# Query splitting spread over two engines, and loads and last products put elsewhere, in a two-layer gated cross-attention kernel

## The chip, the cores and the metric

The kernel runs on one core of one Trainium2 chip. The metric is the device time of one execution in microseconds (us). The engines are called PE (TensorE, with its weight loads listed as PEld), DVE (VectorE), ACT (ScalarE), POOL (GpSimd) and SP (SyncE, which here only issues DMAs). "ACTq" and "SPq" in the profile's rows are the DMA-issuing instructions of ACT and SP.

## The reference

Sixteen samples of 56 queries (width 128) attend to 1500 context rows each, through two layers. Each layer is a gated cross-attention with 16 heads of width 8, followed by a gated mixture of 8 experts:

```
q, k, v = x @ Wq + bq, ctx @ Wk + bk, ctx @ Wv + bv        # split into 16 heads of 8
w   = softmax(q k / sqrt(8))          # layer 1: scores where mask == 0 are -1e9
x   = x + tanh(g_xattn[l]) * (concat(w v) @ Wo + bo)
xf  = layernorm(x)                    # also ahead of q
gate = top-2 of 8, scores softmax (layer 0) or sigmoid (layer 1), normed to sum 1
x   = x + tanh(g_ffn[l]) * sum_e gate[e] * (gelu(xf @ W1[e] + b1[e]) @ W2[e] + b2[e])
```

Layer 0's experts have 512 hidden columns, layer 1's have 64 and there is a shared expert beside them.

## The kernel before

The work is one long pipeline over `NB = 32` batches (16 samples in each of 2 layers), written out as steps `s = -1 .. 35`. A step has 12 places `kt = 0 .. 11`, and every engine's program is an order written by hand over `s` and `kt`; engines meet only through semaphores. In step `s` PE finds the row maxima of batch `s` (24 products into `pMX`, three banks, read by DVE at L1112), computes the scores of batch `s-1` (from kt 3, `pST`, exponentials by ACT at L817), multiplies them with the values (`pO`, L1251), and projects keys of batch `s+1` and values of batch `s` (`pKV`). Everything else of PE goes through one PSUM bank, `pF`, in the order that `f_uses(s)` lists: each use waits until DVE has read the use before it (semaphore `f_free`). The uses that matter here are

- `qT` and `q` (odd steps up to 29, for the next two batches: `has_q`): PE transposes the normalised queries `xnq` and a row `keep` (ones in layer 0, in layer 1 whether a sample has any valid key), and DVE copies both (L1009, L1010). PE then multiplies with Wq and adds the bias through `keepT` (L1393, L1394). DVE makes from the result, for each of the two heads of a pair, the f16 high part (`qhi`, L1020, twice) and the f16 rest (`qlo`, L1022, twice), masked by `head_of`.
- `y` (odd steps, kt 7): the attention's output product (L1335), after `q`. DVE then adds the residual, takes the layer norm's statistics (L1043 to L1049), POOL makes `xnf` (L719 to L724), and PE transposes it at kt 9 (`xT`, L1339) for the experts (`h0` and on, L1404 or L1408).
- `ct` (kt 1): the row maxima of batch `s-1` as f16 rows. SP copies them into `qexp` (L554), and PE's first score tile of that batch, at kt 3, waits for it (`shift_in`).
- `y0` to `y3`, `yb`: the experts' second products and their biases; `gT` the transposed gates. In the last steps (33 = `sums_last`, 34, and 35 = `ends`) these run with nothing beside them.

The f16 parts of the keys are POOL's (`low_part`, three chunks a step, L650 and L652), and so are the parts of the context (L758, L760). In steps 2 and 3 it also makes the low parts of layer 0's first expert weights.

SP issues all loads and copies of the steady state, in program order: in a step first `ct`'s two copies, then key chunk 2, then expert weights (`expert_weights`), the context load (750 KB), key chunk 0, the queries (`queries`, into `qmax`), key chunk 1, and last `late_loads`. In step -1 key chunk 0 stands before the context load, and ACT issues the first queries at kt 5.

## Time and profile before

| | |
|---|---|
| median of 3 runs | 983.31 us (979.77 to 984.18) |
| profiled execution | 990.22 us, of which 988.1 us are the span of the trace |
| mean granted clock of PE in it | 0.954 of full speed |
| busy share of the span | PE 89%, PEld 64%, DVE 72%, ACT 60%, POOL 53% |
| busy us | PE 875.2, DVE 709.9, ACT 591.9, POOL 524.0 |
| DMA queue of SP (q1) | 102.07 MB, 44.2% of 16 engines |

Times within the trace count from the start of the span. The profiled execution is one run and about 7 us longer than the median of the timed ones, so a sum of its durations is compared with its own time, and the difference is carried over to the median.

### The profile page before, as it was taken

To read this page: it belongs to the slowest core of one execution; us is meant where nothing else is said; L and a number is where in the kernel's file an instruction comes from. 1 tells how busy PE (TensorE), PEld (TensorE's weight loads), DVE (VectorE), ACT (ScalarE), POOL (GpSimd) and SP (SyncE) were. 2 spreads that over 40 slices of the span, in tenths; PEclk is the share of its full clock that TensorE was granted. 3 is DMA by queue.
4 is the path that set the end of the run, shared out by engine and by line. 5 is a ranking of instruction groups with operands and counts; after the bars stand their busy time and mean duration, and the time that the engine had idled before them with its cause. 6 is when DMAs were issued, how large, how long until landed. Compare 5 with 4: busy or idle time off the path is not lost.

```text
span 988.1 us, 33064 instructions
## 1 busy us (share of the span) xinstructions
PE 875.2 (89%) x13280; PEld 630.3 (64%) x13280; DVE 709.9 (72%) x1600; ACT 591.9 (60%) x1085; POOL 524.0 (53%) x701
## 2 busy tenths in 40 slices
PE   3888899889898988899999999999999999999975
PEld 1355667667676766667667676666666666666653
DVE  5764885777868586786867858687787878787713
ACT  2254666575665757557575575757666666766560
POOL 5545754536535454463655556677566666662202
PEclk9885998999999999999999999999999999999985
DMA  6243442122222122222666646676786767666200
GB/s 161 84 140 116 136 129 76 53 85 82 77 84 76 47 72 74 84 86 70 122 120 136 147 85 152 135 160 141 147 154 130 161 115 151 134 128 114 44 2 19
DMA packets 103556, 104.49 MB, mean 106 GB/s; under 512 B 28442, under 2 KB 97388, under 8 KB 103404
## 3 DMA queue, kind: packets, MB, share of 16 engines
q1 hardware_dynamic: 101986, 102.07, 44.2%
q8 instruction: 105, 1.72, 0.9%
q10 hardware_dynamic: 1418, 0.32, 0.2%
q14 instruction: 47, 0.39, 0.2%
HBM read 35.89 MB, written 0.46 MB: 37 GB/s over the span
## 4 chain that ended last, share of the span: by engine, by line
PE 56%; DVE 23%; ACT 11%; issue 7%; POOL 2%; DMA 1%; ACTq 0%; SPq 0%; POOLq 0%; DVEq 0%
PE pO L1251 12%; DVE mx L1112 11%; PE pST L1230 10%; PE pMX L1272 9%; PE pKV L1308 5%; PE pKV L1317 5%; ACT P L817 3%; PE pF L1370 3%; PE pF L1404 3%; ACT HR L826 2%; ACT L817 2%; PE pF L1374 2%; DVE HR L994 1%; DVE rden L1038 1%; ACT V L849 1%
## 5 line engine op out<-in xcount | busy, mean ns | idle before, releaser
L1112 DVE TENSOR_REDUCE mx<-pMX 112x1 f32<-112x500 f32 x768 | 489.4, 667 | 110.2 <-PE pMX L1272 106.9
L817 ACT ACTIVATE P<-pST 125x448 f32<-125x448 f32 x768 | 389.5, 542 | 242.8 <-PE pST L1230 239.0
L1230 PE MATMUL pST<-qexp,kop 50*128 50x112 f16 (+2 forms) x3072 | 271.0, 217 | 24.3 <-ACT P L817 15.8
L1272 PE MATMUL pMX<-kop,qmax 48*112 48x500 f16 (+1 forms) x768 | 279.7, 409 | 9.8 <-DMA qmax<-qlo 6.5
L1230 PEld LDWEIGHTS pST<-qexp,kop 50*128 50x128 f16 (+2 forms) x3072 | 185.3, 102 | 104.0 <-ACT P L817 43.1
L1251 PE MATMUL pO<-P,V 125*18 125x112 f32 x6144 | 192.6, 268 | 4.9 <-issue 4.8
L1251 PEld LDWEIGHTS pO<-P,V 125*18 125x18 f32 x6144 | 141.4, 100 | 40.1 <-issue 22.7
L650 POOL CAST khi<-kfull 128x500 f16<-128x500 f32 x96 | 57.7, 601 | 162.3 <-ACT kfull L844 162.1
L1272 PEld LDWEIGHTS pMX<-kop,qmax 48*112 48x112 f16 (+1 forms) x768 | 99.0, 132 | 54.8 <-DVE mx L1112 17.1
L652 POOL TENSOR_TENSOR klo<-kfull,khi 128x500 f16<-128x500 f32 x96 | 109.0, 1135 | 7.8
L760 POOL TENSOR_TENSOR Clo<-C,Chi 128x500 f16<-128x500 f32 x93 | 105.7, 1136 | 7.5
L849 ACT ACTIVATE V<-pKV 125x512 f32<-125x512 f32 x96 | 57.7, 601 | 43.4 <-PE pKV L1317 40.4
L844 ACT ACTIVATE kfull<-pKV,bkp 128x500 f32<-128x500 f32 x48 | 32.5, 677 | 68.0 <-PE pKV L1308 64.4
L1317 PE MATMUL pKV<-Whi,Chi 128*128 128x128 f16 (+1 forms) x384 | 72.0, 225 | 1.3 <-ACT V L849 1.1
L1370 PE MATMUL pF<-w2a,HR 128*112 128x128 f32 x512 | 62.9, 280 | 10.2 <-ACT HR L826 7.9
L1317 PE MATMUL pKV<-Whi,Clo 128*128 128x128 f16 (+1 forms) x384 | 71.4, 223 | 0.0
L1317 PE MATMUL pKV<-Wlo,Chi 128*128 128x128 f16 (+1 forms) x384 | 71.4, 223 | 0.0
L1076 DVE TENSOR_TENSOR ysc<-pF,gate 112x512 f32<-112x512 f32 x32 | 22.1, 692 | 67.8 <-PE pF L1370 49.3
L1370 PEld LDWEIGHTS pF<-w2a,HR 128*112 128x112 f32 x512 | 59.3, 181 | 15.0 <-issue 10.0
L758 POOL CAST Chi<-C 128x500 f16<-128x500 f32 x93 | 55.8, 600 | 12.8 <-PE pKV L1317 10.7
L708 POOL TENSOR_TENSOR OM<-OM,rden 128x112 f32<-128x112 f32 x32 | 13.5, 422 | 86.0 <-DVE rden L1038 86.0
L994 DVE TENSOR_TENSOR HR<-pF,W 128x448 f32<-128x448 f32 x64 | 39.8, 622 | 22.9 <-PE pF L1404 22.2
(161 smaller groups left out, 1199.3 us busy)
## 6 DMA issues: line engine op xcount, KB each, us to landing
C<-in_ctxT SPq DMA_DIRECT2D x31, 750.0 KB, 6.4
kop<-maskop SPq DMA_DIRECT2D x48, 437.5 KB
kop<-khi SPq DMA_DIRECT2D x192, 62.5 KB
kop<-khi SPq DMA_DIRECT2D x96, 125.0 KB
kop<-klo SPq DMA_DIRECT2D x96, 62.5 KB
kop<-klo SPq DMA_DIRECT2D x48, 125.0 KB
maskin<-in_mask SPq DMA_DIRECT2D x8, 656.2 KB, 5.3
qexp<-qmax SPq DMA_DIRECT2D x16, 182.0 KB
```

Of the source, the lines that this page charges most:

```text
L650: nc.gpsimd.tensor_copy(khi[:, cols], kfull[:, c, :]).then_inc(khi_done, 1)
L652: nc.gpsimd.tensor_tensor(klo[:, cols], kfull[:, c, :], khi[:, cols], ALU.subtract).then_inc(klo_done, 1)
L758: nc.gpsimd.tensor_copy(Chi[:, s % 2, cols], C[:, cols]).then_inc(chi_done, 1)
L760: nc.gpsimd.tensor_tensor(Clo[:, s % 2, cols], C[:, cols], Chi[:, s % 2, cols], ALU.subtract).then_inc(ctx_split, 1)
L817: nc.scalar.activation(P[0:KP, slot, h * 4 * T:(h + 1) * 4 * T], pST[0:KP, h, 0:4 * T], ACT.Exp, scale=EXP_SCALE).then_inc(exp_done, 1)
L849: nc.scalar.activation(V[0:KP, s % 2, 4 * c:4 * c + 4, :, 0:PR].rearrange("k t p i -> k (t p) i"), pKV[0:KP, :].rearrange("k (m i) -> k m ...
L1112: nc.vector.tensor_reduce(mx[:, s % 2, c, p:p + 1], pMX[0:T, m % 3, 0:CW], AX.X, ALU.max).then_inc(max_done, 1)
L1230: mm = nc.tensor.matmul(pST[0:keys.stop - keys.start, h, i * T:(i + 1) * T], kop[rows, b, slot, keys], qexp[rows, b, slot, :, :].rearrange ...
L1251: mm = nc.tensor.matmul(pO[32 * g:32 * g + VW, r * T:(r + 1) * T], V[0:KP, b, tile, p, :], P[0:KP, tile % RING, p * T:(p + 1) * T], start= ...
L1272: nc.tensor.matmul(pMX[0:T, m % 3, 0:CW], qmax[rows, b, slot, :, :].rearrange("r j q -> r (j q)"), kop[rows, b, slot, c * CW:(c + 1) * CW] ...
L1317: mm = nc.tensor.matmul(pKV[0:rows, i * D:(i + 1) * D], x_[:, s % 2, cols], m[:, l, 1, :], start=(k == 0), stop=(k == 2))
L1370: mm = nc.tensor.matmul(o, HR[:, F0C * e + c, :], w2a[:, e, c, :], start=(c == 0), stop=(c == F0C - 1))
```

## The change

For the queries, DVE masks both heads in one operation into a new f32 tile `qfull` and frees `pF` with it. POOL makes `qhi` (a cast) and `qlo` (a subtraction) from `qfull`, between its key chunks 1 and 2, and what issues the queries' copies waits for POOL (`q_split`). The row `keep` is transposed and copied in step -1 and for layer 1 alone. Loads: the small ones (`b2x`, `ws2b`, `bs1b`) go from SP's step 1 to ACT's step 0, kt 8; the first mask (656 KB) from SP's step 1 to its step 3; in step -1 the context load stands before key chunk 0. In steps 33 to 35 the experts' second products go into the three banks of `pMX`, under semaphores of their own, in another order; `XF` gets two buffers.

```diff
+def masks_queries(s):
+    return s == -1 or s + 1 >= B
...
     if has_q(s):
-        uses += [(2, "qT", 2), (3, "q", 2)] if s < 0 else [(4, "qT", 2), (6, "q", 2)]
+        uses += [(2 if s < 0 else 4, "qT", 1 + masks_queries(s)), (3 if s < 0 else 6, "q", 1)]
     if has_end(s) and not sums_last(s):
-        uses += [(1, "y2", 0), (2, "y3", 1), (3, "yb", 1)]
+        uses += [(1, "y2", 0), (2, "y3", 1), (3, "yb", 1)] * (not ends(s))
...
-    if sums_last(s):
-        uses += [(5, "y0", 0), (5, "y1", 1), (6, "yb", 1)]
     if has_a(s):
-        uses += [(7, "y", 1)] + [(7, "y2", 0), (7, "y3", 1)] * sums_last(s)
-        uses += [(9, "xT", 1), (10, "h0", 1), (10, "lg", 1), (11, "h1", 1)]
+        uses += [(6 if sums_last(s) else 7, "y", 1), (9, "xT", 1)]
+        uses += [(10, "lg", 1), (10, "h0", 1)] if sums_last(s) else [(10, "h0", 1), (10, "lg", 1)]
+        uses += [(11, "h1", 1)]
...
+def last_uses(s):
+    if sums_last(s):
+        return [(5, "y0", 0), (5, "y1", 1), (7, "y2", 0), (7, "y3", 1), (7, "yb", 1)]
+    if s == NB + 2:
+        return [(10, "y0", 0), (10, "y1", 1)]
+    if ends(s):
+        return [(1, "yb", 1), (2, "y2", 0), (2, "y3", 1)]
+    return []
...
 # SP
             def late_loads(s):
-                if s == 1:
-                    sp.wait_ge(init_w, 4)
-                    sp.dma_start(b2x[0:NE, 0, :], b2_0).then_inc(f_in, 16)
-                    sp.dma_start(b2x[:, 1, :], b2_1).then_inc(f_in, 16)
-                    sp.dma_start(ws2b[:, :], ws2).then_inc(f_in, 16)
-                    sp.dma_start(bs1b[:, :], bs1).then_inc(f_in, 16)
+                if s == 3:
                     sp.dma_start(maskin[:, :], mask[0]).then_inc(mask_in, 16)
...
                 expert_weights(s)
-                if s == -1:
-                    key_chunk(st, 1, 0)
...
                 if has_k(s):
-                    if s >= 0:
-                        key_chunk(st, 1, 0)
+                    key_chunk(st, 1, 0)
                     if has_q(s) and s >= 0:
-                        sp.wait_ge(f_free, st.at(lambda s: upto(f_uses, s, "q", True)))
+                        sp.wait_ge(q_split, 2 * q_count(s) + 2)
...
 # POOL, after low_part(st, 1), the OM and ON products and mask_part(st, 2)
+                if has_q(s):
+                    pool.wait_ge(f_free, upto(f_uses, s, "q", True))
+                    apart(pool)
+                    if s > 0:
+                        pool.wait_ge(qmax_in, q_total(s))
+                        apart(pool)
+                    nc.gpsimd.tensor_copy(qhi[:, :, :, :], qfull[:, :, :, :]).then_inc(q_split, 1)
+                    pool.wait_ge(q_split, 2 * q_count(s) + 1)
+                    nc.gpsimd.tensor_tensor(qlo[:, :, :, :], qfull[:, :, :, :], qhi[:, :, :, :], ALU.subtract
+                                            ).then_inc(q_split, 1)
                 low_part(st, 2)
...
 # ACT
                 if s == -1 and kt == 5:
-                    act.wait_ge(f_free, upto(f_uses, s, "q", True))
+                    act.wait_ge(q_split, 2)
                     queries(act, 0)
...
+                if s == 0 and kt == 8:
+                    act.dma_start(b2x[0:NE, 0, :], b2_0).then_inc(f_in, 16)
+                    act.dma_start(b2x[:, 1, :], b2_1).then_inc(f_in, 16)
+                    act.dma_start(ws2b[:, :], ws2).then_inc(f_in, 16)
+                    act.dma_start(bs1b[:, :], bs1).then_inc(f_in, 16)
...
 # DVE
-                        q = pF[:, 0:T].rearrange("p (b q) -> p b q", b=2)
-                        own = head_of[:, layer_of(s + 1), :]
-                        for j in range(2):
-                            link(nc.vector.tensor_scalar(qhi[:, :, j, :], q, own[:, j:j + 1], None, ALU.mult))
-                        for j in range(2):
-                            nc.vector.scalar_tensor_tensor(out=qlo[:, :, j, :], in0=q, scalar=own[:, j:j + 1],
-                                                           in1=qhi[:, :, j, :], op0=ALU.mult, op1=ALU.subtract
-                                                           ).then_inc(f_free, 1)
+                        q = pF[:, 0:T].rearrange("p (b q) -> p b q", b=2).unsqueeze(2).broadcast_to([128, 2, 2, S])
+                        own = head_of[:, layer_of(s + 1), :].unsqueeze(1).unsqueeze(3).broadcast_to([128, 2, 2, S])
+                        nc.vector.tensor_tensor(qfull[:, :, :, :], q, own, ALU.mult).then_inc(f_free, 1)
...
 # PE, small(use): the last products go to pMX
+                    if is_last(s, use):
+                        into, signal = pMX[:, 2 if use == "yb" else int(use[1]) // 2, :], last_ready
+                        if sums_last(s) and use == "y0":
+                            pe.wait_ge(max_done, NMAX * NB)
+                        if s == NB + 2 and use == "y0":
+                            pe.wait_ge(last_free, before(last_uses, s, True))
```

## Rows read from the trace of the kernel before

**Rows 1.** The page's chain that ended last: shares of the span by engine.
```profile
PE 56%; DVE 23%; ACT 11%; issue 7%; POOL 2%; DMA 1%; ACTq 0%; SPq 0%; POOLq 0%; DVEq 0%
```
**Rows 2.** Instructions grouped by line, shapes apart: total busy us, mean ns | idle before.
```profile
L652 POOL TENSOR_TENSOR klo<-kfull,khi 128x500 f16<-128x500 f32 x96 | 109.0, 1135 | 7.8
...
L650 POOL CAST khi<-kfull 128x500 f16<-128x500 f32 x96 | 57.7, 601 | 162.3 <-ACT kfull L844 162.1
...
L994 DVE TENSOR_TENSOR HR<-pF,W 128x448 f32<-128x448 f32 x64 | 39.8, 622 | 22.9 <-PE pF L1404 22.2
...
L1010 DVE COPY keepT<-pF 1x112 f32<-1x112 f32 x16 | 4.0, 252 | 0.0
...
L1054 DVE TENSOR_TENSOR xflo<-pF,xfhi 128x112 f16<-128x112 f32 x8 | 2.2, 274 | 0.3
```
**Rows 3.** Waits: who waited for whom, us in total, times, longest.
```profile
PE pF L1335 <- DVE qlo L1022: 9.5, 14, 0.9
```
**Rows 4.** Chain in order of time, step 23: start us, us, what.
```profile
707.24 0.41 PE pF L1394 x2
...
709.04 0.69 PE pF L1335 x4
```
**Rows 5.** Timeline of POOL, step 11: start us, us, instruction [idle before <-releaser].
```profile
352.47 1.13 POOL L652 TENSOR_TENSOR klo<-kfull,khi 128x500 f16<-128x500 f32 x1
355.38 0.23 POOL L719 TENSOR_SCALAR vef<-mvf 112x1 f32<-112x1 f32 x1 [1.78 <-DVE mvf L1049]
```
**Rows 6.** Timeline of SP, end of step 1 and start of step 2.
```profile
69.09 0.49 SPq L490 DMA_DIRECT2D b2x<-in_b  x1
...
71.19 0.59 SPq L494 DMA_DIRECT2D maskin<-in_mask  x1
71.89 1.47 SPq L554 DMA_DIRECT2D qexp<-ct  x2
```
**Rows 7.** Timeline of PE, step 2, kt 3.
```profile
77.61 0.61 PE L1230 MATMUL pST<-qexp,kop 50*128 50x112 f16 x8 [5.79 <-issue]
```
**Rows 8.** Windows: us, busy us of each engine (instructions), PE's clock, DMA share, GB/s.
```profile
57.00:71.80 14.80, 13.41 (x251) 9.47 (x250) 12.01 (x26) 10.15 (x21) 6.88 (x8) 1.00 0.39 112
...
77.60:94.50 16.90, 16.75 (x181) 10.87 (x182) 8.21 (x14) 8.79 (x18) 7.67 (x10) 0.50 0.40 130
```
**Rows 9.** Timeline of SP at the end of step 3 and of step 4's `ct`.
```profile
124.66 2.40 SPq L529 DMA_DIRECT2D kop<-khi  x2
128.72 1.36 SPq L554 DMA_DIRECT2D qexp<-ct  x2
```
**Rows 10.** Timeline of PE, step 4, kt 3.
```profile
132.17 0.41 PE L1272 MATMUL pMX<-kop,qmax 48*112 48x500 f16 x1
```
**Rows 11.** Timeline of all engines, step -1 and start of step 0.
```profile
12.50 2.86 ACTq L467 DMA_DIRECT2D qmax<-qhi  x4
...
14.10 1.13 POOL L652 TENSOR_TENSOR klo<-kfull,khi 128x500 f16<-128x500 f32 x1
...
15.15 0.51 SPq L581 DMA_DIRECT2D C<-in_ctxT  x1
...
21.20 1.05 PE L1272 MATMUL pMX<-kop,qmax 48*112 48x500 f16 x3 [6.54 <-DMA qmax<-qlo]
```
**Rows 12.** DMA issues by line: KB each, median us from issue to landing.
```profile
out<-X SPq DMA_DIRECT2D x1, 56.0 KB, 1.6
```
**Rows 13.** Chain in order of time, steps 33 to 35: start us, us, what.
```profile
957.12 0.46 PE pF L1330 x2
...
962.63 0.71 PE pF L1354 x2
...
963.76 1.21 PE pF L1335 x4
...
968.76 0.46 PE pF L1339
...
979.63 0.70 DVE ysc L1076
```

85 lines of the change are left out of this document (59 added, 26 removed).

## The prediction

> **What bounds the kernel now.** I read the page's chain of the work that ended last first: PE 56%, DVE 23%, ACT 11% [rows 1]. So there is no single bound, and an edit is worth what it takes off that chain where it stands. Next I asked for the waits of PE. One recurs: the output product `y` waits for DVE's `qlo`, 14 times, once in each odd step from 3 to 29, for 9.5 us, 0.68 us each [rows 3]. The chain in order of time shows the place: in step 23 PE ends the query product at 707.65, the next piece of PE is `y` at 709.04, and the 1.39 us between are DVE's four query operations [rows 4]. In layer 0 the chain goes on through DVE and POOL to the experts, and POOL starts `vef` when DVE's statistics are ready, 1.78 us after it had nothing to do [rows 5].
>
> Then I looked for single long holes. The longest in the steady state is 5.79 us of idle PE in step 2, at kt 3, before the first score tile of batch 1 [rows 7]. "Issue" says that the profile names no releaser. That tile needs the copies of `ct`. SP was free for them at 69.09, but first issued five late loads, the 656 KB mask last at 71.19, and only at 71.89 the copies [rows 6], which then follow the mask in the same queue. The windows show what came behind: PE at its 2.4 GHz level before the hole (granted 1.00), at its 1.2 GHz level for 16.9 us behind it (granted 0.50), busy 16.75 of them [rows 8]. The start waits for the last `qmax<-qlo` copy until 21.20 [rows 11], and the end is one serial chain through `pF` [rows 13].
>
> **The change part by part.** Every term is in us on the profiled execution (990.22); minus is a gain.
>
> *Query operations, steps 5 to 29.* One operation of 224 columns takes the place of four. A `tensor_tensor` from PSUM takes 0.274 for 112 columns and 0.622 for 448 [rows 2], by a line between them 0.39 for 224; ends 0.27 and 0.62. With the hand-overs some 0.45 stand where 1.39 stood, so `pF` is free 0.9 earlier. PE, however, idles only 0.68 of this time; the rest is its own work, so `y` comes 0.68 earlier. POOL takes over a cast and a subtraction of 224 columns. For 500 columns it needs 0.60 and 1.135 [rows 2]. In proportion that is 0.27 + 0.51 = 0.78, at the full price 1.74. Fixed costs weigh more in short operations: I take 0.95, and 0.05 for hand-over. They stand ahead of key chunk 2, so this moves: in step 11 `klo` ended at 353.60 and `vef` started at 355.38 [rows 5]. With the pair from 351.95 (DVE's result at 351.86) to 352.95 and chunk 2's 1.8 behind it, POOL is free at about 354.8, and starts `vef` there, 0.55 earlier instead of 0.9. So layer 0's five steps (5 to 13) give 0.55 each, -2.8. In layer 1 the chain behind `y` is PE itself [rows 4], and the eight steps 15 to 29 give 0.68 each, -5.4. The pair's results are needed by the next step's first product, five places later; SP's issue waits about 0.1 longer than before, which nothing on the chain sees.
>
> *Step 1* has no `y`; behind the query operations stand the row maxima, -0.7. *Step 3* goes the other way: POOL has four expert parts there and is itself on the chain, so its pair comes on top, +1.0 (0.8 to 1.7).
>
> *Row of ones.* Six odd steps of layer 0 behind step 1 and step 1 itself lose a copy of 0.25 [rows 2] and a transposition. The copy stands between the transposition and PE's `sum`; I count 6 times 0.25, -1.5 (0 to -2.2).
>
> *Small loads to ACT.* Four issues of about 0.5 [rows 6]. ACT has nothing to do at that place of step 0 until the values' products are ready: 0. Uncovered they would cost 2.
>
> *The mask away from step 1.* With all five issues gone, `ct`'s copies are issued at about 69.2 and take 1.47. A small copy with a free queue lands 1.6 after its issue [rows 12]; the second is issued at 70.0, so both are there by 71.8, when PE asks: -5.8 for the hole. What is late next is nothing but PE's own pace. The time at half clock: 251 matmuls took 14.8 at full clock [rows 8], so the 181 of the 16.9 us would take 10.7, which is 6.2 less. As ACT and DVE don't get faster with PE, I take -5.5 (0, if the clock falls anyway, to -6.2).
>
> *The mask in step 3.* SP now issues it at 127.1, behind key chunk 1, and `ct`'s copies of step 4 at 128.72 [rows 9] queue behind it. In step 2 PE went on 6.42 after the mask's issue [rows 6, 7]. The same gives 133.5, and PE is at this tile at about 132.2 [rows 10], since four expert products fill the places before: +1.3 (0 to 4).
>
> The Trainium skill ("DMA: Bandwidth & Descriptors", "Issuing engines are not separate DMA queues") says that transfers share the same 16 DMA engines whoever issues them, so a load given to ACT saves only the issuing time. By that rule the gain is the mask's move in time and not the change of queue, and it would be as large with the small loads left on SP but for their 2 us of issue.
>
> *Start.* POOL makes the first query parts only behind key chunk 1, which it ends at 15.23, so at about 16.3; ACT's six issues, from 12.50 at 0.72 each [rows 11], start 3.8 later and end at 20.6, and behind them key chunk 2 is late too, which has slack until kt 8. But the last copy lay behind the context load issued at 15.15 [rows 11], which now is gone by then. With a landing of 1.6 after the last issue [rows 12] it is there at 21.5 to 22.3, against 20.96: +1.0 (0 to 3.8, if something else holds it).
>
> *End.* PE no longer waits for `rden`, the read of `ysc` and the bias ahead of `y`: `sum` ends at 957.58, two groups of four products of 1.2 [rows 13] follow, and `y` starts at about 960.5, not 963.76. But `y2`, `y3` and `yb` (2.5 + 1.5, the bias products being two pairs of 0.7) now stand ahead of `xT`, which so comes at 965.8, not 968.76 [rows 13]: -3.0. Behind it, dropping one read of `ysc` (0.70) and of `gateT` pays for the bias products that were moved forward. Together -3.0 (-2 to -4).
>
> Sum: -2.8 - 5.4 - 0.7 + 1.0 - 1.5 - 5.8 - 5.5 + 1.3 + 1.0 - 3.0 = -21.4, from 990.22 to 968.8. The profiled execution is 6.9 above the median of the three runs. Carried over, 983.3 - 21.4 = 962.
>
> **The rivals.** *The hole moves, or the clock stays.* The mask holds `ct` in step 4 as it did in step 2 and PE falls to half clock there, or it does so in step 2 for another reason. For it: a lull of PE was followed by the low level once [rows 7, 8]. Against it: PE gets to step 4's tile late. The 5.5 are lost: 968.
>
> *POOL becomes the bound of the odd steps.* If the pair costs 1.74, `vef` in layer 0 comes 0.2 later than before instead of 0.55 earlier, and in layer 1 PE waits for `xT` likewise. Fourteen steps lose about 1.0 of the forecast each: 976. Against it: the idle 1.78 before `vef` [rows 5].
>
> *The mask was not the cause.* The copies are late because of something the rows don't name. Then 11.3 stay: 973. Against it is only the order in the queue.
>
> *Slower.* POOL's pair alone decides it, where it is on the chain in all 14 odd steps. To lose the 21.4 and 5 more, each step must lose 1.9 more than forecast, so the pair must take some 2.9 and not 1.0: 989. Nothing in the rows is that slow at this size; the full price of 500 columns is 1.74.
> The Trainium skill ("GPSIMD Engine Reference", "4.1 Engine selection") speaks against this part: elementwise work on two inputs belongs on VectorE, being about twice as slow on GpSimd. By that rule the subtraction costs more in total busy time than it saves; whether it costs time is a question of which engine waits.
>
> *No effect.* DVE's time comes back in another wait of the same step, and the hole's in the next step: within 5 of 983.
>
> **How the numbers follow.** A measurement of this kernel tells about 0.5% (4.9) from no change. Chances: the sum as it stands 0.52 (955 to 968), clock or second hole 0.20 (968), POOL 0.14 (976), mask innocent 0.07 (973), no effect 0.04, slower 0.03. The likeliest gives 962. Upward the range takes the bounds of the clock (5.5), the start (2.8) and half of POOL's case, to 975; downward the bounds at the start, in step 4 and at the row of ones (3), `y`'s full 0.9 (3), and 3 from run to run, to 953. Faster 0.93, same 0.04, slower 0.03.
>
> **What would show it.** Right: no wait of PE for DVE before `y`; one DVE line of about 0.4 for the queries and two POOL lines summing to 0.95; no idle PE at step 2's kt 3 and a granted clock of 1.00 there; a hole of 1 to 2 at step 4's kt 3; the first row-maximum product at about 22; the last stretch from `sum` to the end shorter by 3. Wrong: POOL's `vef` released by POOL's own queue later than before; half clock in steps 2 to 4; step lengths from one step's maxima to the next's in layer 1 that stay as they are.

## The result and the profile after

The kernel after takes 967.19 us (median of 4 runs, 965.04 to 972.72); the kernel before took 983.74 on the same chip (979.77 to 985.60). The ratio is 0.985, with a 95% interval of 0.980 to 0.990: faster by 16.5 us. The predicted 962 is 5 us too low, and 967 lies in the range. The profiled execution of the kernel after took 965.04, with a span of 963.2; that of before took 990.22, with a span of 988.1. The two profiled spans lie 24.9 apart, because the one of before lies 6.5 above the median of its kernel and that of after 2 below. So I compare steps and not totals.

A step is measured from the DVE reduction `m` of one step's row maxima to that of the next. Where nothing disturbs them, equal steps agree to 0.04 us, also between kernels. Each length is from one profiled execution. The start and steps 1 to 3 scatter more: the four traces of kernels that make their first queries as the kernel after does have a start of 42.17 to 42.75. The lengths, in us:

| | before | after | difference | forecast |
|---|---|---|---|---|
| start, to the first `m` | 41.87 | 42.17 | +0.30 | +1.0 |
| step 1 | 24.87 | 24.20 | -0.67 | -0.7 |
| step 2 | 32.97 | 22.42 | -10.55 | -11.3 |
| step 3 | 25.22 | 29.03 | +3.81 | +0.75 |
| step 4 | 30.16 | 30.00 | -0.16 | +1.3 |
| steps 5 to 31 | 779.55 | 766.68 | -12.87 | -9.45 |
| of these, an odd step of layer 0 | 28.34 | 27.83 | -0.51 | -0.80 |
| an odd step of layer 1 | 28.19 | 27.71 | -0.48 | -0.68 |
| last `m` to the end | 53.42 | 48.72 | -4.70 | -3.0 |

(The forecast has the row of ones in it, -0.25 in each odd step from 3 to 13.) In steps 5 to 31 the thirteen odd steps give 5 x 0.51 + 8 x 0.48 = 6.4. The other 6.5 goes, but for 0.3 in step 31, with TensorE's clock: the trace of before shows seven stretches there at the 1.2 GHz level, one of 6.8 us and six of 3.4, and that of after four of 3.4. A step with one of 3.4 is 1.2 to 1.6 us longer than its equals, the one with 6.8 is 2.7 longer. The stretches sit elsewhere, or are absent, in kernels whose steps there are the same. Without them the differences of the table add up to 18.4, near the 16.5 of the medians.

The waits of PE and POOL after; columns: who waited for whom, us in total, times, longest.

```profile
PE pF L1391 <- POOL xnf L749: 6.3, 8, 2.6
POOL qhi L734 <- DVE qfull L1059: 15.6, 15, 4.5
POOL vef L744 <- DVE mvf L1090: 6.2, 2, 3.4
```

The wait of `y` for DVE [rows 3] is no longer among them: it was 9.5 us in 14 waits. A smaller one stands in its place. `xT` waits for POOL's `xnf` for 6.3 us in 8 waits. `vef`, for which DVE's statistics came last in step after step of before [rows 5], waits for them in two steps only. POOL in step 11, timeline:

```profile
339.00 0.37 POOL L734 CAST qhi<-qfull 128x224 f16<-128x224 f32 x1 [1.21 <-DVE qfull L1059]
339.44 0.61 POOL L736 TENSOR_TENSOR qlo<-qfull,qhi 128x224 f16<-128x224 f32 x1
340.00 0.60 POOL L665 CAST khi<-kfull 128x500 f16<-128x500 f32 x1
340.68 1.14 POOL L667 TENSOR_TENSOR klo<-kfull,khi 128x500 f16<-128x500 f32 x1
341.78 0.24 POOL L744 TENSOR_SCALAR vef<-mvf 112x1 f32<-112x1 f32 x1
```

The idle 1.78 us ahead of `vef` [rows 5] is used up; the five stand back to back. The new operations by themselves, grouped by line (total busy us, mean ns):

```profile
L1059 DVE TENSOR_TENSOR qfull<-pF,head_of 128x224 f32<-128x224 f32 x16 | 6.3, 392 | 10.3 <-PE pF L1451 10.3
...
L736 POOL TENSOR_TENSOR qlo<-qfull,qhi 128x224 f16<-128x224 f32 x16 | 9.7, 609 | 1.3
...
L734 POOL CAST qhi<-qfull 128x224 f16<-128x224 f32 x16 | 5.9, 372 | 15.6 <-DVE qfull L1059 15.6
```

The pair costs 0.98 us (0.95 estimated), the operation on DVE 0.39 (0.39).

SP at the turn from step 1 to step 2, timeline; the answer to [rows 6]:

```profile
69.75 1.37 SPq L572 DMA_DIRECT2D qexp<-ct  x2
```

The last copy of `ct` landed at 72.14, 1.7 us after the issue of the second (70.48), and PE idles 0.21 us there. In the kernel before it had landed at 77.52, 4.9 us after its issue (72.67), and PE went on at 77.61 [rows 7]. The windows of step 2, of step 3 to its stretch at half clock, and of that stretch (us, busy us and instructions of PE, PEld, DVE, ACT and POOL, then PE's clock, DMA share, GB/s):

```profile
66.40:88.80 22.40, 18.88 (x354) 12.77 (x352) 17.53 (x32) 16.59 (x34) 13.86 (x17) 1.00 0.42 125
88.80:112.00 23.20, 18.55 (x321) 12.95 (x322) 18.74 (x39) 15.09 (x30) 18.00 (x25) 1.00 0.51 147
112.00:115.40 3.40, 3.40 (x51) 2.54 (x49) 1.32 (x3) 0.55 (x1) 2.87 (x4) 0.51 0.18 50
```

PE is at its 2.4 GHz level through step 2, where the kernel before had 16.9 us at a granted 0.50 [rows 8]. Step 3, however, has 3.4 us at the 1.2 GHz level, from 111.95, which is 1.7 us behind the end of PE's longest idle time there. That idle time and its cause are in POOL's timeline of step 3 and PE's row behind it:

```profile
103.29 0.37 POOL L734 CAST qhi<-qfull 128x224 f16<-128x224 f32 x1 [0.20 <-DVE qfull L1059]
103.73 0.61 POOL L736 TENSOR_TENSOR qlo<-qfull,qhi 128x224 f16<-128x224 f32 x1
...
106.07 2.26 POOL L675 TENSOR_TENSOR w1lo<-HR,w1hi 128x512 f16<-128x512 f32 x2
108.31 0.23 POOL L744 TENSOR_SCALAR vef<-mvf 112x1 f32<-112x1 f32 x1
```
```profile
110.25 0.29 PE L1391 MATMUL pF<-ident,xnf 112*128 112x112 f32 x1 [2.60 <-POOL xnf L749]
```

PE's second longest idle time of step 3 is at its first product, which needs the query rows. SP's row of their last copies, and PE's:

```profile
86.36 1.24 SPq L490 DMA_DIRECT2D qmax<-qlo  x2
```
```profile
89.06 0.39 PE L1316 MATMUL pMX<-kop,qmax 48*112 48x500 f16 x1 [1.48 <-DVE mx L1153]
```

The row names DVE, but the last of these copies landed at 88.86, 0.20 us ahead of the product, and in the twelve kernels in which this product waits, those below included, it starts 0.20 us or 0.21 behind that landing. So I take the copy as the releaser. In the kernel before the rows landed at 95.78 and the product started at 98.35, without a wait.

The chain of the end, in order of time (start us, us, what):

```profile
937.83 1.05 PE pMX L1429 x4
938.93 1.19 PE pMX L1429 x4
940.12 1.14 PE pF L1387 x4
...
943.92 0.83 POOL xnf L749
944.75 0.14 issue
944.88 0.43 PE pF L1391
```

From the last `m` to `xT` it was 34.1 us and is 30.4.

### The profile page after: what moved, and what is told of

Its sections match the earlier page's. It is cut to its first block, busy times and chain, and to the rows that moved or that the text cites. A ratio compares the mean times of both kernels' runs of the same rounds, so it can differ in the third digit from the quotient of the medians.

```text
span 963.2 us, 33056 instructions
## 1 busy us (share of the span) xinstructions
PE 861.1 (89%) x13273; PEld 620.4 (64%) x13273; DVE 697.7 (72%) x1545; ACT 591.7 (61%) x1085; POOL 538.8 (56%) x733
## 4 chain that ended last, share of the span: by engine, by line
PE 56%; DVE 20%; ACT 11%; issue 6%; POOL 3%; ACTq 1%; DMA 1%; SPq 0%; POOLq 0%; DVEq 0%
PE pO L1295 12%; PE pST L1274 11%; DVE mx L1153 10%; PE pMX L1316 9%; PE pKV L1361 5%; PE pKV L1352 5%; ACT P L856 3%; PE pF L1425 3%; PE pF L1461 3%; ACT HR L865 2%; ACT L856 2%; DVE HR L1033 1%; ACT V L888 1%; DVE rden L1078 1%; ACT L865 1%
## 5 line engine op out<-in xcount | busy, mean ns | idle before, releaser
L1274 PE MATMUL pST<-qexp,kop 50*128 50x112 f16 (+2 forms) x3072 | 268.2, 215 | 19.8 <-ACT P L856 16.6
L1274 PEld LDWEIGHTS pST<-qexp,kop 50*128 50x128 f16 (+2 forms) x3072 | 182.8, 100 | 99.1 <-ACT P L856 42.6
L1295 PE MATMUL pO<-P,V 125*18 125x112 f32 x6144 | 189.4, 265 | 4.5 <-issue 4.4
L1295 PEld LDWEIGHTS pO<-P,V 125*18 125x18 f32 x6144 | 139.2, 99 | 39.1 <-issue 19.8
L1425 PE MATMUL pF<-w2a,HR 128*112 128x128 f32 x512 | 61.2, 275 | 10.6 <-ACT HR L865 8.0
L1117 DVE TENSOR_TENSOR ysc<-pF,gate 112x512 f32<-112x512 f32 x28 | 19.4, 692 | 58.0 <-PE pF L1425 49.2
```

Source lines behind the costliest of these rows:

```text
L1274: mm = nc.tensor.matmul(pST[0:keys.stop - keys.start, h, i * T:(i + 1) * T], kop[rows, b, slot, keys], qexp[rows, b, slot, :, :].rearrange ...
L1295: mm = nc.tensor.matmul(pO[32 * g:32 * g + VW, r * T:(r + 1) * T], V[0:KP, b, tile, p, :], P[0:KP, tile % RING, p * T:(p + 1) * T], start= ...
L1425: mm = nc.tensor.matmul(o, HR[:, F0C * e + c, :], w2a[:, e, c, :], start=(c == 0), stop=(c == F0C - 1))
```

## The experiments

Twelve kernels ran. Their step lengths stand together, since most verdicts are read from them (us; "odd 0" and "odd 1" are an undisturbed odd step of either layer; the total is the median, with the number of runs). "wait 3" is PE's wait at the first product of step 3, "low 3" the time at the 1.2 GHz level in step 3. e1 to e4, e5 to e8 and e9 to e12 ran on three chips, each with the kernel before beside them (medians 983.3, 982.5 and 981.7), so ratios compare better than totals:

| | start | 1 | 2 | 3 | wait 3 | low 3 | 4 | odd 0 | odd 1 | end | total |
|---|---|---|---|---|---|---|---|---|---|---|---|
| before | 41.87 | 24.87 | 32.97 | 25.22 | 0 | 0 | 30.16 | 28.34 | 28.19 | 53.42 | 983.7 (4) |
| after | 42.17 | 24.20 | 22.42 | 29.03 | 1.48 | 3.4 | 30.00 | 27.83 | 27.71 | 48.72 | 967.2 (4) |
| e1_mask_only | 42.59 | 26.88 | 22.16 | 31.17 | 3.60 | 10.2 | 30.00 | 28.35 | 28.19 | 52.41 | 981.9 (10) |
| e2_small_only | 43.06 | 26.96 | 21.83 | 30.40 | 2.77 | 10.2 | 30.00 | 28.34 | 28.19 | 53.14 | 980.3 (10) |
| e3_q_only | 45.03 | 26.64 | 28.85 | 29.54 | 0 | 6.8 | 30.00 | 27.86 | 27.72 | 52.91 | 983.1 (10) |
| e4_dve_splits_two | 39.14 | 23.87 | 21.87 | 30.25 | 2.29 | 10.2 | 30.00 | 27.83 | 27.71 | 48.54 | 963.4 (4) |
| e5_w1lo_behind | 42.60 | 26.69 | 21.60 | 28.46 | 2.84 | 3.4 | 31.75 | 27.82 | 27.71 | 48.23 | 971.0 (1) |
| e6_weights_late | 39.93 | 23.67 | 22.79 | 28.47 | 0.17 | 3.4 | 30.00 | 27.83 | 27.71 | 48.62 | 968.1 (1) |
| e7_dve_splits_all | 40.56 | 26.89 | 21.59 | 28.40 | 2.61 | 3.4 | 30.00 | 30.11 | 28.83 | 47.72 | 996.1 (4) |
| e8_pair_behind | 40.26 | 23.60 | 23.54 | 32.36 | 2.05 | 13.7 | 30.00 | 27.54 | 27.48 | 48.75 | 989.5 (10) |
| e9_mask_back | 42.75 | 26.60 | 22.98 | 29.70 | 2.11 | 6.8 | 30.00 | 27.83 | 27.71 | 48.23 | 964.3 (1) |
| e10_small_back | 42.42 | 23.60 | 26.47 | 30.83 | 0.37 | 10.2 | 29.99 | 27.82 | 27.71 | 48.48 | 970.4 (1) |
| e11_three_in_two | 40.24 | 23.54 | 21.81 | 29.23 | 0.72 | 3.4 | 30.00 | 27.82 | 27.71 | 47.74 | 964.1 (6) |
| e12_three_on_dve | 39.64 | 24.44 | 21.99 | 26.08 | 1.53 | 0 | 31.68 | 27.99 | 27.88 | 48.49 | 962.5 (4) |

Step 1 comes in two lengths, 23.5 to 24.9 and 26.6 to 27.0. They go with TensorE's clock: the stretch at 1.2 GHz that begins at the end of the start is over by 57.3 us or earlier in before, after, e4, e6, e8 and e12 (13.7 long), and at 65 to 67 in e1, e3 and e9 (20.5 long). Kernels with the same step 1 stand on both sides (after and e5), so I don't put it down to an edit. It matters all the same, because the longer step 1 brings PE later to step 2's first tile of batch 1, where the hole of the kernel before is.

The length of step 3 follows "low 3" closely: 25.2 and 26.1 with none, 28.4 to 29.2 with 3.4 us, 29.5 and 29.7 with 6.8, 30.3 to 31.2 with 10.2, 32.4 with 13.7. Waits and the low clock go together here, and this order alone doesn't say which brings which. In e5 and e12 a stretch of 3.4 us falls in step 4, which is 1.7 longer, so steps 3 and 4 have to be read together.

**e1_mask_only and e2_small_only** put one half each of the moved loads into the kernel before.

```
 e1:            if s == 1: ... four small loads
-                   sp.dma_start(maskin[:, :], mask[0])
+               if s == 3:
+                   sp.dma_start(maskin[:, :], mask[0])
 e2:            if s == 1:
-                   ... four small loads
                    sp.dma_start(maskin[:, :], mask[0])
+ ACT, step 0, kt 8:  the four small loads
```

> The kernel before with only the first mask load moved from SP's step 1 to its step 3; the four small loads stay ahead of ct's copies. Theory (the mask ahead of ct's copies in SP's queue made the hole of step 2): the copies are issued 0.7 us earlier, at about 71.2, with a free queue, and PE goes on at about 73.7, so the hole shrinks from 5.8 to about 2 us; if PE keeps its high clock behind it, step 2 is 8 to 9 us shorter than before (32.97 us in the trace before), otherwise 4. Time 973 to 976 (980 if the clock falls). Rival (the hole has another cause, or SP's issue time of all five loads is what counts): the hole stays at 5 us or more and the time within 1 us of before. Step 4 should be no longer than before, or up to 1.3 us if the mask now delays ct there.

> The kernel before with only the four small loads moved to ACT's step 0; the mask stays at SP's step 1, ahead of ct's copies. Theory (mask in the queue): the mask is issued at about 69.1 and PE goes on some 6.4 us later, at 75.5; the hole is 3.7 us instead of 5.8 and PE still falls to its low clock, so step 2 is 2 us shorter and the time 981 to 982. Rival (SP's issue time is what counts): the hole nearly vanishes, step 2 is 8 to 10 us shorter and the time 974.

In both traces the hole is nearly gone (0.53 and 0.20 us), and step 2 is 22.16 and 21.83 for 32.97. Part of this is when PE arrives: step 1 has its longer length here, and PE reaches the tile at 74.55 and 75.10, for 71.82 in before. e10 and e9 below have the same loads ahead of `ct` as e1 and e2, with holes of 2.50 and 1.35. So these two traces don't show that either half alone cures a PE that comes at 71.8. And though step 2 gained more than was expected of either, the totals gained little: e1's 981.9 is 2 over the most that its theory allowed, and e2's 980.3 is near its theory's, with a step 2 like its rival's. e1 stands at a ratio of 0.9996 to before (0.9965 to 1.0028), e2 at 0.9966 (0.9930 to 1.0001). Of e1's 10.8 us in step 2, 6.0 come back in step 3 and 2.0 in step 1; e2 loses 5.2 in step 3, 2.1 in step 1 and 1.2 at the start (the part in step 1 goes with the clock there and is not put down to the edit). The waits of PE in step 3 of e1 show what took the place of the hole, a wait for the query rows at the step's first product:

```profile
PE pMX L1273 <- DMA qmax<-qlo: 3.6, 1, 3.6
```

In e1 SP's queue issues with no gap over 0.2 us from 70.02 until these rows are out at 92.1; in the kernel before it stood still from 80.8 to 86.1. The stall was cover for SP's queue. The second thing lost is clock: e1 has 10.2 us at 1.2 GHz from 92.2, e2 from 92.8.

**e3_q_only** put the query operations alone into the kernel before (DVE's one operation, POOL's pair and their waits; not the context load, the small loads, the mask, the row of ones or the end).

> The kernel before with only the query split changed (one masking operation on DVE, cast and subtraction on POOL). Theory (POOL's pair of 1.05 us now ends last in every odd step): the start of vef is 0.48 us earlier relative to the query operation's start in each odd step from 5 to 29, whatever the layer, and each of these steps 0.48 us shorter, -6.2 together; step 3 longer by 1.2 us or more; the first row maximum product 1 to 4 us later, as the context load still stands in the way of the last query copy. Time 979 to 982. Rival (PE's wait for pF was the whole effect, as forecast): 0.68 us in the steps of layer 1, -8.2 and 977.

The odd steps shorten by 0.48 in layer 0 and 0.47 in layer 1, the same in both layers. What else moved gives it back: the start is 3.2 us longer (2.4 against e1, whose start is that of before), step 1 is 1.8 longer, and step 3 is 4.3 longer while step 2 is 4.1 shorter. Step 2 is shorter with all five loads in place because PE, after the longer step 1, reaches the tile at 76.75 and waits 3.56 us, not 5.79. Step 3 is the other thing to note: there is no wait for the query rows, and POOL's pair alone brings PE's wait for `xnf` from 0.5 to 2.6 us, with 6.8 us at 1.2 GHz behind it. The ratio is 0.9987 (0.9954 to 1.0021). The pair's cost at the start is 2.4 to 3.2 us when the context load is where it was. The kernel after, with the loads reordered, has +0.3. Against the odd steps of the kernel after (27.83 and 27.71) those of e3 are 0.03 and 0.01 longer. In layer 1 the row is copied in both, so what the row of ones gives in layer 0 is 0.03 at most.

**e4_dve_splits_two** is the kernel after, with DVE making the parts itself in steps -1 and 3, from `qfull`.

```
-                if has_q(s):                                   # POOL
+                if has_q(s) and s not in (-1, 3):
 ...
                 nc.vector.tensor_tensor(qfull, q, own, ALU.mult)
+                if s in (-1, 3):
+                    nc.vector.tensor_copy(qhi, qfull)
+                    nc.vector.tensor_tensor(qlo, qfull, qhi, ALU.subtract)
```

> The changed kernel, where in steps -1 and 3 DVE makes the f16 parts itself, from qfull (a cast and a subtraction behind the masking), and POOL does in all other odd steps. Theory (in step 3 POOL's pair is on the chain, 1.2 us, and the gap of PE behind it drops the clock): step 3, 29.03 us in the trace after, falls to 25.5 to 27.5; in step -1 the query copies are issued 3 us earlier, and the first row maximum product starts 2 to 3 us earlier unless key chunk 0, which lands behind the context load, ends last. Time 2 to 5 us under the changed kernel, 962 to 965. Rival (step 3 is long for the C load, the expert loads or DVE): step 3 stays at 29 and the time at that of the changed kernel.

The total is 963.4, a ratio of 0.9791 (0.9730 to 0.9852), within the 962 to 965 expected, but of the two reasons given only one came true. The start is 3.0 shorter. Step 3 is not: 30.25. Taking POOL's pair out of step 3 was not enough, because a wait of 2.3 us for the query rows, one of 1.5 for DVE's maximum and 10.2 us at half clock stand there:

```profile
PE pMX L1328 <- DMA qmax<-qlo: 2.3, 1, 2.3
PE pMX L1328 <- DVE mx L1165: 1.5, 1, 1.5
```

**e5_w1lo_behind** takes, in the kernel after, the two `w1lo` operations of step 3 from ahead of `vef` to behind `xnf`.

```
                 low_part(st, 2)
-                expert_low(st, 2); expert_low(st, 3)
+                if s != 3: expert_low(st, 2); expert_low(st, 3)
                 ... vef, rsf, xnf
+                if s == 3: expert_low(st, 2); expert_low(st, 3)
```

> The kernel after, with one thing moved: in step 3 GpSimd makes the low parts of experts 6 and 7 (w1lo, 1.15 us each) behind vef, rsf and xnf and not ahead of them. In the kernel after, step 3 is 29.03 us long where it was 25.22 before, TensorE stands 2.6 us ahead of xT behind GpSimd's xnf, and vef starts 2.2 us after the last DVE operation it needs (mvf ends at 105.70, vef starts at 108.31). Theory, GpSimd bounds step 3: xT comes 2.1 to 2.3 us earlier against the step's start and step 3 falls to about 26.8 (25.9 to 27.2). Rival, the length of step 3 is set at its entry, by query rows and clock: TensorE's wait ahead of xT goes but the step stays at 28.5 to 29.5 because another wait behind it takes its place. Steps 5 to 29 stay at 27.8 and 30.1 in layer 0.

It gave 0.57 instead of 2.2, and step 4 is 1.75 longer, with a stretch at 1.2 GHz in it. The idle time ahead of `xT` did go, from 2.60 to 0.4. The expert products wait for the very `w1lo` that was moved. The wait for the query rows at the step's first product is not new, but it is 2.84 for 1.48, though up to there the two programs are the same: the rows landed 2.7 us after their last issue, not 1.9.

```profile
PE pMX L1320 <- DMA qmax<-qlo: 2.8, 1, 2.8
...
PE pF L1465 <- POOL w1lo L675: 1.6, 1, 1.6
```

So moving POOL's work inside the step did not help here: the rival was nearer the truth. It is one trace, and what differs in it without an edit behind it (the landing, the clock) is as large as the effect that was looked for.

**e6_weights_late** issues, in e4, the three expert weight loads of step 2 behind the query rows.

```
-                expert_weights(s)
+                if s != 2: expert_weights(s)
                 ... context load, key chunk 0, query rows
+                if s == 2: expert_weights(s)
```

> The version in which VectorE makes the parts of steps -1 and 3 (e4), with one thing moved: in step 2 SyncE issues the three loads of expert weights (1.5 us of issuing, 768 KB) behind the key chunk and the query rows and not ahead of them. In e4 the queue of SyncE issues without a gap from 66.6 to 84.5, and the first pMX product of step 3 waits 2.3 us for the query rows; in the run with the mask alone moved it waits 3.6 us. Theory, the stall of step 2 was cover for SyncE's queue, and without it the query rows of step 3 are late by what is issued ahead of them: they leave 1.5 us earlier and land 1.5 to 2.5 us earlier, the wait at the entry of step 3 falls from 2.3 to under 1 us, and step 3 falls from 30.25 to 28 to 29. Rival, the landing is what is slow, by the bytes of the context load and the weights, or the wait is replaced by one for VectorE's maximum: the wait stays over 1.5 us or step 3 stays over 29.5.

Step 3 falls from 30.25 to 28.47, as expected, and the wait at its first product from 2.29 to 0.17. e11, which has the weights late too, has 0.72. In the nine kernels with a hole of 1.35 us or less and the weights in their old place it is 1.5 to 3.6, in e10, with a hole of 2.5, 0.37, and in before and e3, with holes of 5.8 and 3.6, nothing. So SP's queue is what makes this wait, and the stall was what covered it. PE's waits for DVE are now the longest of step 3 (2.6 us in five waits).

**e7_dve_splits_all** is e4 with the parts made by DVE in every step, again from `qfull`.

> The kernel after, but VectorE makes the two f16 parts in every step, from the masked queries, with one cast and one subtraction over all 224 columns; GpSimd makes none. Theory, the pair on GpSimd bounds vef of each odd step (0.98 us ahead of klo, vef right behind klo), and the pair is no gain over three wide operations on VectorE: vef comes at +3.3 to +3.7 us from the start of the masking operation (after: +3.44), the steps 5 to 29 keep their length within 0.3, the start is 3 us shorter (39.1 for 42.2), and the total is 962 to 965, 2 to 5 us under the kernel after. Rival, VectorE bounds: its queue carries 0.6 to 0.9 us more in each odd step, as it did before the change, vef comes at +3.9 as before, the odd steps go back to 28.3 in layer 0, 28.2 in layer 1 (+0.5 x 13), and the total is 967 to 970.

996.1 us, a ratio of 1.0146 (1.0076 to 1.0217): 29 over the kernel after, far worse than the theory's 962 to 965 and the rival's 967 to 970. The odd steps are 30.11 and 28.83 where nothing else disturbs them. The timelines of DVE and of POOL in step 11 show why.

```profile
356.88 0.39 DVE L1063 TENSOR_TENSOR qfull<-pF,head_of 128x224 f32<-128x224 f32 x1 [0.59 <-PE pF L1463]
357.31 0.64 DVE L1068 CAST qhi<-qfull 128x224 f16<-128x224 f32 x1
357.98 1.29 DVE L1070 TENSOR_TENSOR qlo<-qfull,qhi 128x224 f16<-128x224 f32 x1
```
```profile
357.21 0.60 POOL L669 CAST khi<-kfull 128x500 f16<-128x500 f32 x1 [0.89 <-ACT kfull L887]
357.89 1.13 POOL L671 TENSOR_TENSOR klo<-kfull,khi 128x500 f16<-128x500 f32 x1
```

DVE's cast ends 0.14 us behind POOL's `khi`, its subtraction 0.25 behind POOL's `klo`: each is stretched until POOL's operation is over. Step -1 has the same subtraction with POOL idle:

```profile
12.02 0.39 DVE L1070 TENSOR_TENSOR qlo<-qfull,qhi 128x224 f16<-128x224 f32 x1
```

In the fifteen others, all beside `klo`, it takes 1.21 to 1.30 us. The Trainium skill ("SBUF — State Buffer", "SBUF: two separate sides") says that a DVE operation in a two-port mode, or one with two SBUF inputs beside a GpSimd operation that reads SBUF, contends with GpSimd for one pair of ports, an exclusive lock: whichever starts first has it for its whole length, and the other waits. The trace agrees, with 1.29 us beside POOL for 0.39 alone.

**e8_pair_behind** puts POOL's pair, in e4, behind `xnf` (except in steps -1 and 3, where DVE makes it).

> The version in which VectorE makes the parts of steps -1 and 3 (e4), with one thing moved: in the other odd steps GpSimd makes the pair behind vef, rsf and xnf and not ahead of the last key chunk's parts. Theory, the pair is on the path of GpSimd ahead of vef: with it gone vef waits for VectorE's mvf (+3.06 us from the masking operation) and starts at about +3.1, not +3.44, xT comes 0.3 to 0.4 us earlier and each of the 12 odd steps gets 0.3 to 0.4 shorter, 27.5 for 27.8, total 4 us under e4 (958 to 961). Rival, the query rows leave 2.5 to 3 us later, SyncE's queue and the first pMX products of the next step wait for them: the even steps get longer by 1 to 3 us each, total 975 or more.

Both halves of the expectation happened. The odd steps are shorter by 0.29 and 0.23, as POOL's bound before `vef` says. The even steps are longer, 31.1 for 30.25 in layer 0, 39.85 for 33.98 in step 16 and 26.5 to 27.7 for 25.58 in layer 1, and the total is 989.5, a ratio of 1.0054 (1.0016 to 1.0093). The query rows now leave late, and what stands behind them in SP's queue too. In step 11 SP issues them from 348.33; m of that step is at 353.22. In the kernel after the same issue starts at 340.43 and `m` is at 349.86, so the margin shrank from 9.4 to 4.9 us. Behind them key chunk 1 and `ct` shift likewise. Between 607 and 690 us (steps 20 to 22) PE waits 4.2 us, in two waits, for scores whose copies are late: both products start 0.09 us behind the landing of `ct`'s last copy.

```profile
PE pST L1286 <- issue: 4.2, 2, 2.1
```

**e9_mask_back and e10_small_back** take the kernel after and put back one half each of the loads in step 1, ahead of `ct`'s copies.

```
 e9:   late_loads:
-                if s == 3:
+                if s == 1:
                    sp.dma_start(maskin[:, :], mask[0])
 e10:  late_loads:
+                if s == 1:
+                    ... four small loads      (gone from ACT)
                 if s == 3:
                    sp.dma_start(maskin[:, :], mask[0])
```

> The kernel after, with the mask load back in step 1, ahead of the copies of ct in SyncE's queue; the four small loads stay on ScalarE in step 0. In the kernel before, the last copy of ct landed at 77.52, 4.9 us after its issue began (72.67), and TensorE stood until 77.61; in the kernel after it landed at 72.14, 1.7 us after its issue (70.48), and TensorE never waited. With the mask as the only late load in the queue (the run with the small loads alone moved) it landed 1.9 us after its issue. Theory of the prediction, the mask's packets are served ahead of the copies of ct: the last copy lands 4 us or more after its issue, TensorE stands 2 to 4 us at key tile 3 of step 2, and step 2 is 24.5 to 27 us (22.42). Rival, it takes the mask and the small loads together, by issue time and landing: the copies land in 1.7 to 2.2 us and step 2 stays within 0.7 us of 22.4.

> The kernel after, with the four small loads back in step 1 in SyncE's queue, ahead of the copies of ct; the mask stays in step 3. Theory of the prediction, their 2.4 us of issuing matter little beside the mask: the copies of ct are issued 1 to 2 us later than in the kernel after (69.75), land in under 2.2 us, and step 2 is 22.4 to 23.4. Rival, the small loads fill the queue: step 2 is over 24.5 us. In step 3 the query rows land about as much later as the queue is behind, up to 2.4 us, so its length may grow by 0 to 2.4.

SP's timeline of e9, then PE at the place of the hole:

```profile
69.91 1.31 SPq L512 DMA_DIRECT2D maskin<-in_mask  x1
71.91 1.37 SPq L572 DMA_DIRECT2D qexp<-ct  x2
```
```profile
75.78 0.37 PE L1274 MATMUL pST<-qexp,kop 50*128 50x112 f16 x7 [1.35 <-issue]
```

The same of e10, and its windows around the wait:

```profile
70.81 0.60 SPq L516 DMA_DIRECT2D bs1b<-in_bs  x1
71.53 1.45 SPq L578 DMA_DIRECT2D qexp<-ct  x2
```
```profile
74.08 0.61 PE L1275 MATMUL pST<-qexp,kop 50*128 50x112 f16 x8 [2.50 <-issue]
```
```profile
66.00:73.30 7.30, 5.10 (x99) 3.17 (x96) 5.58 (x11) 4.13 (x8) 2.13 (x3) 1.00 0.20 59
73.30:80.10 6.80, 5.88 (x65) 3.74 (x65) 2.73 (x6) 3.19 (x7) 1.84 (x2) 0.50 0.23 72
```

With the mask alone ahead of them the copies landed 3.0 us after their issue (75.69 for 72.64), 0.24 behind the mask itself (75.45), and PE waited 1.35; step 2 is 0.56 longer. (In before the mask landed at 76.89 and the copies at 77.52.) Neither expectation of e9 is met: the landing lies between the two. For e10 the rival's is, a step 2 over 24.5. With the small loads alone they landed 1.7 after their issue (74.00 for 72.30), but were issued 1.8 later than in the kernel after, PE waited 2.50, fell to 1.2 GHz for 6.8 us, and step 2 is 4.05 longer. One difference between the two has to be kept in mind: step 2 began at 66.0 in e10 and at 69.4 in e9, so PE reached the tile earlier in e10 (71.59) than in e9 (74.44). So the hole of the kernel before has two causes, late issue by the small loads and late landing by the mask, and the first was not in the prediction as a cause of its own. PE came at 71.82 in before, nearly as in e10, so an estimate from e10's 2.50 leaves some 3.3 of the 5.8 us to the mask; no trace shows that share by itself. Step 3 is longer than in the kernel after as well, by 0.67 and 1.80.

**e11_three_in_two and e12_three_on_dve** let DVE make the parts straight from PSUM, so that no operand pair comes from SBUF: one operation for `qhi` with the mask broadcast, two for `qlo`. e11 does so in steps -1 and 3 (and has the late weights of e6), e12 in every step, with no pair on POOL at all.

```
 e12:  link(nc.vector.tensor_tensor(qhi, q, own, ALU.mult))          # q: PSUM, broadcast
       for j in range(2):
           nc.vector.scalar_tensor_tensor(out=qlo[:, :, j, :], in0=q1, scalar=own1[:, j:j + 1],
                                          in1=qhi[:, :, j, :], op0=ALU.mult, op1=ALU.subtract)
```

> The kernel after, with two changes meant to take back what step 3 and the start lost: in steps -1 and 3 VectorE makes the parts itself, straight from PSUM, in three operations (qhi with the broadcast mask, then qlo for each head group), and in step 2 SyncE issues the expert weights behind the query rows. Elsewhere GpSimd's pair stays. Theory, parts made from PSUM don't suffer where parts made from SBUF did (qhi 0.72 and qlo 1.30 us in step 3 of the run with the late weights): the three take 1.0 to 1.1 us, the start is 39.0 to 40.0 (42.17 after), step 3 is 27 to 28 (29.03 after), steps 5 to 29 as in the kernel after but for changes of clock, total 959 to 963. Rival, step 3's length is set at its entry and by the clock, and what is saved there is given back: step 3 stays over 28.4 and the total is within 2 us of the version of e4 (963.4).

> The kernel after, but GpSimd makes no parts at all: in every query step VectorE makes them from PSUM in three operations (one broadcast for qhi, two for qlo), where the kernel before used four. The run in which VectorE made both parts from SBUF had odd steps of 30.1 in layer 0 and 28.8 in layer 1, with a subtraction of 1.29 us that ended 0.2 us after GpSimd's klo. Theory, it was reading both operands from SBUF while GpSimd ran that cost, and not VectorE's load: here the three take 1.0 to 1.1 us, vef starts at +3.6 to +3.7 from the first of them (after +3.44, before +3.93), the odd steps are 28.0 to 28.2 in layer 0 and 27.9 to 28.1 in layer 1, 0.2 to 0.3 over the kernel after, the start is 39 to 40, and the total is 965 to 970. Rival, VectorE's queue bounds as soon as it makes the parts: odd steps of 28.8 or more and a total of 975 or more.

e12 takes 962.5 us, a ratio of 0.9806 to before (0.9757 to 0.9855), 2.5 under the least that was expected; e11 964.1, a ratio of 0.9808 (0.9768 to 0.9848). The two intervals overlap with that of the kernel after (0.980 to 0.990), so it is the steps that set e12 apart. Its three operations take 1.00 us from first to last, in DVE's timeline of step 3:

```profile
99.67 0.39 DVE L1049 TENSOR_TENSOR qhi<-pF,head_of 128x224 f16<-128x224 f32 x1 [0.67 <-PE pF L1445]
100.09 0.58 DVE L1051 SCALAR_TENSOR_TENSOR qlo<-pF,head_of,qhi 128x112 f16<-128x112 f32 x2
```

Its odd steps are 27.99 and 27.88, at the low edge of what was expected and only 0.16 longer than with GpSimd's pair, and its start is 2.5 shorter. Its step 3 is 2.95 shorter, but its step 4 is 1.68 longer, since the stretch of 3.4 us at 1.2 GHz falls there (from 116.19): steps 3 and 4 together are 1.27 shorter. In e11 step 3 did not come down: 29.23, with one wait of 1.8 us ahead of a score product at 93.00 and 3.4 us at half clock from 94.9. Its theory failed for step 3; the start is 40.24, 0.2 over what it said. That is the rival of e11, as is the total within 2 us of e4's. What set that wait was not tried.

## Why the prediction was right, point by point

**Right in direction and size.** The hole of step 2 and its clock gave 10.6 of the forecast 11.3, and the pair on POOL and the operation on DVE cost what was estimated (POOL's subtraction takes 609 ns, where DVE took 0.39 us for it in e7 with POOL idle). Step 1 gave 0.67 of 0.7, but among the seven traces of after and of its variants with the shorter step 1 it scatters from 23.54 to 24.44, so this figure confirms nothing. The total lies in the range, and that it came within 5 us is in part luck: the misses listed at the end are 6.8 us one way and 3.9 the other. The range itself was added up wrongly at the top: 962 + 5.5 + 2.8 + 7 is 977, not 975.

**The stall's cause was half told.** "Five late loads, the 656 KB mask last" was right. e9 and e10 split them: either half makes a hole by itself, and how large depends on when PE comes, as e3's 3.56 for 5.79 with the same loads shows. The prediction took the mask for the gain and priced the small loads at "their 2 us of issue" if left on SP. e10 contradicts this price: step 2 was 4.05 longer for it, with a wait of 2.50 and 6.8 us at 1.2 GHz. What the Trainium skill says ("DMA: Bandwidth & Descriptors", "Issuing engines are not separate DMA queues"), that transfers share the same 16 DMA engines whoever issues them, isn't touched by that; the price that was drawn from it is.

**Step 3 was the step that failed.** Its term was +1.0 for the pair, and +0.75 with the row of ones; it measured +3.8. Two things were missing. First, the stall of step 2 had let SP's queue get ahead. Without it the query rows of step 3 are late: PE waits 3.6 us (e1) to 1.5 (e12, and the kernel after itself) at the step's first product, and moving 1.5 us of issue behind them takes the wait away (e6). The forecast had this at nothing ("What is late next is nothing but PE's own pace"). In e1 and e2, whose query operations are the old ones, this and the clock alone make step 3 5 to 6 us longer. Second, the clock: 3.4 us at the 1.2 GHz level fall in step 3 where before has none. The pair itself cost about its term in one comparison and more in another. e12, which has every other edit of the kernel after, has steps 3 and 4 together at 57.76, for 59.03 after and 55.38 before: 1.3 for the pair, 2.4 for what the two share, the wait of 1.5 and a stretch at 1.2 GHz. e3, with the pair and without the wait, has 59.54, 4.2 over before, with 6.8 us at 1.2 GHz. So how the 3.8 divide is not settled. That the hole's time comes back "in the next step" stood among the rivals, in *No effect*, with 0.04; it is nearly what happened to e1 and e2, and a third of it in the kernel after.

**The odd steps: POOL is the bound in both layers.** Layer 0 was forecast at 0.55 and gave 0.51 (0.48 in e3, which has none of the other edits). Layer 1 was forecast at 0.68, "the chain behind `y` is PE itself", and gave 0.48: POOL's queue, not PE, releases `vef` there too. That is 8 x 0.20 = 1.6 us too much. e8 confirms the bound by taking the pair away from there, with a gain of 0.29 and 0.23 more.

**The row of ones** gave 0.03 per step at most, not 0.25: e3 against the kernel after. The copy was not on the path. 1.3 us of the forecast's 1.5 were not there.

**The mask in step 3** cost nothing in step 4; +1.3 was forecast. SP issued it at 116.98, 0.8 us ahead of `m` (117.82), where the estimate had it 2.2 behind. The copies follow only 4.4 us later, so the mask had landed (121.91) when they were on their way; they landed at 123.80, and PE has no idle time there. Part of this is chance, since the longer step 3 moved `m` behind the mask's issue. But e12, with its short step 3, issues the mask at 114.32, 2.2 us behind `m` as forecast, its copies land at 119.21, and PE starts the tile at 120.90 without a wait. It comes there 1.5 us later than usual, after a stretch at 1.2 GHz, but the copies, 7.07 us behind `m`, would have been just in time for its usual 7.07 to 7.24. So the term comes to about nothing in the forecast's own timing too. SP's timeline in the kernel after:

```profile
116.98 0.58 SPq L512 DMA_DIRECT2D maskin<-in_mask  x1
121.43 0.67 SPq L572 DMA_DIRECT2D qexp<-ct  x1
```

**The start** took +0.3, not +1.0, which is within its scatter: the first row-maximum product begins at 21.34, for 21.20 [rows 11]. The reorder of the context load pays for the pair (e3, without it: +2.4 to +3.2). The pair still costs some 2.5 there: the start is 42.17 to 42.75 in the four kernels that have it and the reorder, and 39.14 to 40.56 in the six in which DVE makes these parts.

**The end** gave 4.7, not 3.0. `xT` comes 3.7 us earlier, and the chain shows POOL's `xnf` ahead of it, not the products `y2`, `y3` and `yb` in PE's queue, which the forecast put there. Another 1.0 came behind `xT`, where the forecast had the reads and the bias products even out.

In sum, without the changes of clock behind step 4: +0.30 - 0.67 - 10.55 + 3.81 - 0.16 - 6.4 - 4.70 = -18.4, for the forecast's -21.4. The misses are step 3 (3.1 too good), layer 1 (1.6), layer 0 with the row of ones (1.4), step 2 (0.7), and against them the end (1.7), step 4 (1.5) and the start (0.7).

## What to carry to other kernels

A stall that everybody waits out is also time in which queues run ahead. When it is removed, ask which queue (here SP's, at 0.6 us an issue) is the next to be late, and look at the step behind it before the gain is counted. Work handed from one engine to another must be priced by who is the bound in each stage: against three operations on VectorE the pair on GpSimd saved 0.16 us in each of 13 steps, and cost some 2.5 at the start and 1.3 in steps 3 and 4. By these steps the version without the pair is the better one by 1.7 us, which the totals' intervals can't tell. Compare equal steps of two traces, not spans: at 0.04 us they show what 1% of scatter in the total hides. But do so only where steps are undisturbed: a stretch at the low clock can move from one step into the next and pass for a gain. And when a wait's releaser had long been done, look for the landing that comes just ahead of its end.

## What the runs showed of the hardware that was not expected

DVE operations with both operands in SBUF, and some casts and scalar operations with one there, end only behind a GpSimd operation that was running when they began, however small they are. In the kernel after, of those that began with over 0.25 us of the GpSimd operation left, this holds for `cc<-m` 11 times of 11, for `cc<-cc,m` 9 of 9 and for `XF` 7 of 7. The first, `cc<-m`, 8 columns, takes 0.17 us at the median of its 32 times. In step 3 it took 0.93 and ended with POOL's subtraction, in the timelines of DVE and of POOL:

```profile
89.01 0.93 DVE L1169 TENSOR_SCALAR cc<-m 112x8 f16<-112x8 f32 x1
89.97 0.50 DVE L1170 SCALAR_TENSOR_TENSOR cc<-cc,m 112x8 f16<-112x8 f16 x1
```
```profile
88.78 1.13 POOL L794 TENSOR_TENSOR Clo<-C,Chi 128x500 f16<-128x500 f32 x1
```

Not every operation on SBUF is stretched: the reduction `m` starts at 88.79, beside the same `Clo`, and takes 0.18 us, as in all its 32 times, and the norm's statistics (`stf`, `mvf`) ended ahead of GpSimd's operation 14 times of 14. Nor is one that reads PSUM: `qlo` from PSUM takes 329 ns for 112 columns, before and in e12 alike, 30 times of 32 beside a GpSimd operation, where the subtraction from SBUF in e7 goes from 0.39 to 1.30 for 224. And TensorE's clock makes waits dearer than they are long: in e10 a wait of 2.50 us came with 6.8 us at 1.2 GHz, and the step is 4.05 longer than in the kernel after.
